# Eight tiles of the second block computed in seven products instead of eight

## What is computed

```
scale = cond @ norm_w.T + 1.0
h = x * (scale * rsqrt(mean(x*x) + EPS))          # x: 4 x 1024 x 512
val, gate = split(h @ up_w.T)                     # up_w: 4096 x 512
h = val * gelu(gate)                              # exact gelu, 2048 wide
h = act_quant(h)                                  # per row: 127 / max|h|, rounded
y = h @ weight_quant(down_w).T + x                # scale 1 / mean|down_w|, rounded to -1, 0, 1
```

## Time and profile before

| what | value |
|---|---|
| median of 3 runs | 761.38 us |
| the profiled execution's own time | 760.18 us |
| its span | 758.4 us |
| PE busy | 736.5 us (97%) |
| DVE busy | 546.8 us (72%) |
| ACT busy | 344.9 us (45%) |
| POOL busy | 96.1 us (13%), all of it before 245 us |

### The profile page before, as it was taken

How to read it: one execution, slowest core, us unless ns; L and a number is a source line. 1 busy time by engine, 2 the same in 40 slices (tenths; PEclk the granted TensorE clock), 3 DMA queues, 4 the chain that set the end, 5 groups by cost and what they waited for, 6 DMA issues and landing times.

```text
span 758.4 us, 15668 instructions
## 1 busy us (share of the span) xinstructions
PE 736.5 (97%) x6190; PEld 611.2 (81%) x6218; DVE 546.8 (72%) x1070; ACT 344.9 (45%) x672; POOL 96.1 (13%) x134
## 2 busy tenths in 40 slices
PE   3999999999999999999999999999999999999998
PEld 2888889888678887888768887788878887688864
DVE  5567777887688776878667775777758776377747
ACT  4788766444255442554235432444315343233325
POOL 0101377773323000000000000000000000000000
PEclk9999999999999999999999999999999999999999
DMA  8787674656546444343533435343343333453302
GB/s 313 275 277 224 197 258 139 223 170 220 207 133 192 152 148 154 115 140 99 175 124 115 129 113 166 105 149 127 126 160 101 99 98 115 130 170 98 103 29 83
DMA packets 43785, 116.63 MB, mean 154 GB/s; under 512 B 4928, under 2 KB 5184, under 8 KB 42432
## 3 DMA queue, kind: packets, MB, share of 16 engines
q1 hardware_dynamic: 43712, 115.63, 46.9%
HBM read 98.83 MB, written 16.78 MB: 152 GB/s over the span
## 4 chain that ended last, share of the span: by engine, by line
PE 85%; DVE 5%; ACT 3%; issue 3%; DMA 2%; POOL 0%; SPq 0%; DVEq 0%; ACTq 0%
PE ps_v L519 15%; PE ps_v L520 15%; PE ps_v L521 15%; PE ps_y L613 12%; PE ps_g L520 8%; PE ps_g L521 8%; PE ps_g L519 8%; PE ps_v L677 1%; DMA q<-in_up_t_dram 1%; DMA sums<-in_up_t_dram 1%; ACT w_hi L758 1%; DVE x_lo L999 1%; ACT g L720 1%; ACT w_hi L763 1%; DVE xt L975 1%
## 5 line engine op out<-in xcount | busy, mean ns | idle before, releaser
L519 PE MATMUL ps_v<-x_hi,w_hi 128*128 128x256 f16 x1216 | 332.0, 273 | 5.3 <-DVE x_lo L999 2.4
L521 PE MATMUL ps_v<-x_hi,w_lo 128*128 128x256 f16 x1216 | 332.0, 273 | 0.0
L520 PE MATMUL ps_v<-x_lo,w_hi 128*128 128x256 f16 x1216 | 332.0, 273 | 0.0
L519 PE MATMUL ps_g<-x_hi,w_hi 128*128 128x256 f16 x640 | 174.6, 273 | 0.0
L520 PE MATMUL ps_g<-x_lo,w_hi 128*128 128x256 f16 x640 | 174.5, 273 | 0.0
L521 PE MATMUL ps_g<-x_hi,w_lo 128*128 128x256 f16 x640 | 174.4, 273 | 0.0
L702 ACT COPY ps_g<-ps_v 128x256 f32<-128x256 f32 x96 | 34.3, 357 | 231.7 <-PE ps_v L521 231.7
L519 PEld LDWEIGHTS ps_v<-x_hi,w_hi 128*128 128x128 f16 x1216 | 119.2, 98 | 23.3 <-DVE ps_g L1005 2.8
L520 PEld LDWEIGHTS ps_v<-x_lo,w_hi 128*128 128x128 f16 x1216 | 119.1, 98 | 16.0
L521 PEld LDWEIGHTS ps_v<-x_hi,w_lo 128*128 128x128 f16 x1216 | 119.2, 98 | 14.0
L713 ACT ACTIVATE g<-ps_g,w_unscale 128x512 f32<-128x512 f32 x128 | 87.3, 682 | 68.2 <-PE ps_g L521 68.1
(11 more groups left out here) (109 smaller groups left out, 579.4 us busy)
## 6 DMA issues: line engine op xcount, KB each, us to landing
w_lo<-w_lo_dram SPq DMA_DIRECT2D x96, 448.0 KB, 3.3
q<-in_up_t_dram SPq DMA_DIRECT2D x16, 512.0 KB, 5.4
xt<-in_x_cols_dram SPq DMA_DIRECT2D x8, 1024.0 KB, 5.1
res<-in_x_rows_dram SPq DMA_DIRECT2D x26, 256.0 KB, 3.5
out_dram<-res SPq DMA_DIRECT2D x26, 256.0 KB, 2.8
sums<-in_up_t_dram SPq DMA_DIRECT2D x12, 512.0 KB, 4.8
xs<-in_x_rows_dram SPq DMA_DIRECT2D x22, 256.0 KB, 3.5
w_lo_dram<-w_lo SPq DMA_DIRECT2D x16, 256.0 KB, 4.8
```

Source lines behind the costliest of these rows:

```text
L519: pe.matmul(to, w_hi[:, wh:wh + P], hi, start=start and kt == 0, stop=False, skip_group_check=True)
L520: pe.matmul(to, w_hi[:, wh:wh + P], lo, start=False, stop=False, skip_group_check=True)
L521: last = pe.matmul(to, w_lo[:, wl:wl + P], hi, start=False, stop=(kt == 1), skip_group_check=True)
```

## The change

Four things change.

**Seven products from tile 24 on** (`S_FIRST` = 24 in place of 32). The activations of block 1 get their sums (`made(1)` has eight operands, three low parts and four differences more on DVE, four high parts more on ACT, in steps 9 to 15), and tiles 8 to 15 of the weight sums come first (`SUM_ORDER`), at steps 14 to 24, the other eight at steps 25 to 33. Sixteen sums as before.

**Memory.** The down weights' raw parts move from `sums` to the part of `w_lo` that holds sums of weights, so `sums` is free from the start and POOL does sums and down parts in turn (`DOWN_AT`). The third place of a sum is `res`. `load_xt(2)` moves from step 14 to 16, and the 1 MB of rows of block 3 are loaded behind it in one piece into `q`, in place of four loads of 256 KB.

**Head.** The first block's rows are loaded in two halves, one more of their sums of squares goes from DVE to ACT, `weight_high(0)` comes before `weight_bound(1)`, two low parts are made on POOL (`low_first`), `weight_scale(1)` comes before `low(0, XB21)`, and the products of tile 0 are reordered.

**Bounds.** The turn of a weight's peak is a bf16 matmul against a bf16 identity in place of an fp32 transpose, and `weight_bound(j)` waits for the clamp, not for the turn.

```diff
-    SUM_AT = (20, 21, 22, 23, 24, 25, 26, 27, 28, 30, 31, 33, 34, 36, 37, 39)
-    SUM_PLACE = (2, 3, 0, 2, 1, 0, 3, 1, 0, 1, 0, 1, 0, 1, 0, 1)
+    S_FIRST = J + J // 2
+    SUM_ORDER = (*range(J // 2, J), *range(J // 2))
+    SUM_AT = (14, 15, 17, 18, 20, 21, 23, 24, 25, 26, 27, 28, 29, 30, 32, 33)
+    SUM_PLACE = (0, 1, 0, 1, 0, 1, 0, 1, 2, 0, 1, 2, 0, 1, 0, 1)
...
     def in_seven(n):
-        return n >= 2 * J
+        return n >= S_FIRST
...
+        if c == 1:
+            return (XB11, XB12, XT1, XT2, XT3, XB21, XB22, XN4)
...
-    LOAD_DOWN_AT = (10, 10, 11, 11, 11, 12, 12, 14, 15, 16, 17, 17, 18, 18, 18, 19)
-    LOW_DOWN_AT = (12, 13, 14, 15, 15, 16, 16, 16, 17, 17, 18, 18, 18, 19, 19, 20)
+    LOAD_DOWN_AT = (11, 11, 10, 10, 11, 12, 12, 14, 15, 15, 16, 16, 17, 18, 18, 18)
+    DOWN_AT = (11, 11, 12, 12, 13, 14, 15, 15, 15, 16, 17, 18, 18, 18, 19, 20)
+    LOW_DOWN_AT = (12, 13, 13, 14, 14, 15, 16, 16, 16, 17, 18, 19, 19, 19, 20, 21)
...
-        down_raw = [res[:, 0, :], res[:, 1, :], *[sums[:, k * D:(k + 1) * D] for k in range(4)],
+        down_raw = [res[:, 0, :], res[:, 1, :], *[w_lo[:, k * WL + WA:(k + 1) * WL].bitcast(F32) for k in range(LS)],
...
+        xs_fourth = q[:, 8 * TB:16 * TB].bitcast(F32)
...
-            return {1: 1, 2: 9, 3: J - 1, 4: 2 * J + 11}.get(c, (c - 2) * J + 6) + i
+            return {1: 1, 2: 9, 3: J + 1, 4: 2 * J + 11}.get(c, (c - 2) * J + 6) + i
...
-                if n == J - 2:
+                if n == J:
                     load_xt(2)
+                    sp.wait_ge(w_ready, J)
+                    sp.dma_start(xs_fourth, x_rows[3]).then_inc(xs_fourth_loaded, 16)
...
-                turn(j % 2, peak[:, j % 2:j % 2 + 1]).then_inc(w_rows, 1)
+                pe.matmul(ps_y[:, 1, (j % 2) * P:(j % 2 + 1) * P], peak_top[:, j % 2:j % 2 + 1].to_broadcast([P, P]),
+                          ident_top, start=True, stop=True).then_inc(w_rows, 1)
...
             def sum_high(k):
+                j = SUM_ORDER[k]
                 act.wait_ge(s_step, 4 * (k + 1))
-                act.wait_ge(val_ready, J + min(k + 2, J))
+                act.wait_ge(val_ready, j + 2 if J + j + 1 >= S_FIRST else J + j + 2)
...
             square(0, 0)
             square(0, 1)
+            square(0, 2)
             weight_bound(0)
+            weight_high(0)
             weight_bound(1)
-            weight_high(0)
...
+            low_first(XB12)
+            low_first(XB22)
-            for n in range(J):
+            for n in range(SUM_AT[-1]):
...
-            for k in range(J):
-                sum_weights(k)
+                for k in range(J):
+                    if n + 1 == SUM_AT[k]:
+                        sum_weights(k)
+                for k in range(J):
+                    if n == DOWN_AT[k]:
+                        quantize_down(k)
...
+                    if j == 9:
+                        difference(1, XT1)
+                        difference(1, XT2)
                     if j == 10:
                         low(1, XB11)
                         low(1, XB12)
                     if j == 11:
+                        difference(1, XT3)
+                        low(1, XT1)
+                    if j == 12:
+                        difference(1, XN4)
+                        low(1, XT2)
+                    if j == 13:
+                        low(1, XT3)
                         low(1, XB21)
+                    if j == 14:
                         low(1, XB22)
+                    if j == 15:
+                        low(1, XN4)
```

More of the change, by code:

```diff
@@ L210, in bass_cond_norm_geglu_bitlinear @@
         up_loaded = [sem(f"up_loaded{k}") for k in range(RS)]
-        sum_loaded = [sem(f"sum_loaded{k}") for k in range(4)]
+        sum_loaded = [sem(f"sum_loaded{k}") for k in range(3)]
         down_sum_loaded = [sem(f"down_sum_loaded{k}") for k in range(4)]
@@ L325, in sum_raw @@
             place = SUM_PLACE[k]
[L326 to L329, removed]
+            if place == 2:
+                return res[:].rearrange("p a n -> p (a n)")
+            return sums[:, place * WS:(place + 1) * WS]
         def sum_loads(k):
@@ L375, in load_lo @@
                 if in_seven(n):
-                    if n < 2 * J + LS:
-                        last = max(k for k in range(J) if SUM_PLACE[k] == 2 + (n % LS) // 2)
-                        sp.wait_ge(ws_ready, last + 1)
-                    if n < 3 * J:
-                        stored, count = sum_store(j)
+                    if n < S_FIRST + LS:
+                        sp.wait_ge(dw_ready, LS + 6 + n % LS)
+                    if n < S_FIRST + J:
+                        stored, count = sum_store(SUM_RANK[j])
                         sp.wait_ge(stored, count)
@@ L438, in _ @@
             sp.dma_start(norm_sb, norm_t).then_inc(consts_loaded, 16)
-            sp.dma_start(xs_first, x_rows[0]).then_inc(xs_first_loaded, 16)
+            for half in range(2):
+                sp.dma_start(xs_first[:, half * 2 * D:(half + 1) * 2 * D],
+                             x_rows[0][:, half * 2 * D:(half + 1) * 2 * D]).then_inc(xs_first_loaded[half], 16)
             load_up(0)
@@ L536, in direct_first @@
                 product(n, OA11, XB11, ps_g[:, n % NG, :], 0, start=True)
+                if n == 0:
+                    product(n, OA21, XB12, ps_v[:, n % NV, :], 1)
                 product(n, OA11, XB12, ps_g[:, n % NG, :], 1)
@@ L734, in square @@
                     tile = xs_third[:, i * D:(i + 1) * D]
+                elif c == 3:
+                    act.wait_ge(xs_fourth_loaded, 16)
+                    tile = xs_fourth[:, i * D:(i + 1) * D]
                 else:
@@ L812, in _ @@
                     if j == 10:
+                        high(1, XT1)
+                        high(1, XT2)
+                    if j == 11:
+                        high(1, XT3)
                         high(1, XB21)
+                    if j == 12:
                         high(1, XB22)
+                    if j == 13:
+                        high(1, XN4)
+                if n == S_FIRST + 1:
+                    high(2, XN4)
                 for k in range(J):
@@ L826, in _ @@
                         high(b + 1, XB22)
-                        high(b + 1, XN4)
+                        if b >= 2:
+                            high(b + 1, XN4)
                 for c in range(1, NB):
@@ L978, in difference @@
             def difference(c, k):
-                before = (c - 2) * 4
+                before = (c - 1) * 4
                 if k == XT1:
@@ L1093, in _ @@
             dve.tensor_scalar(cs[:], cs_raw, cs_scale[:], None, ALU.mult).then_inc(cs_scaled, 1)
-            for i in range(2, TT):
+            for i in range(3, TT):
                 tile = xs_first[:, i * D:(i + 1) * D]
-                dve.wait_ge(xs_first_loaded, 16)
+                dve.wait_ge(xs_first_loaded[i // 2], 16)
                 dve.scalar_tensor_tensor(out=tile, in0=tile, scalar=1.0, in1=tile, op0=ALU.mult, op1=ALU.mult,
@@ L1105, in _ @@
             low(0, XB11)
-            low(0, XB12)
             norm(0, 2)
             norm(0, 3)
+            weight_scale(1)
             low(0, XB21)
-            low(0, XB22)
             for n in range(NJ + 2):
@@ L1115, in _ @@
                     row_scales(b - 1)
-                if b == 0 and j + 1 < J:
+                if b == 0 and 1 <= j < J - 1:
                     weight_scale(j + 1)
```

90 lines of the change are left out of this document (57 added, 33 removed).

## The result

The changed kernel takes 771.06 us (median of 4 runs, 770.25 to 772.19) against 760.93 us for the kernel before (4 runs): ratio 1.014, 95% interval 1.0128 to 1.0152. It is 10.1 us slower. The forecast was 761.7 with a range of 755.8 to 766.0, so it was wrong, and on the slow side. The profiled execution took 770.89 us, with a span of 768.8 in place of 758.4.

The account below looks back on a forecast made before the run. PE bounds the kernel before; VectorE in steps 14 to 31 would turn PE's 7.0 us gain into waits. PE 1.9 us later at tile 32, less 1.6 after, gives + 0.3: 760.5 profiled, median 761.7, range 755.8 to 766.0.

Parts of the forecast that it names:

- The head and the bounds: Tile 0's earlier start was to give 1.0 us, the cheaper turns of bounds in block 0 0.7 us.
- The saving of the seven products: On PE, eight tiles at 4.58 in place of 5.24 us a step: 5.3 us less PE work.
- After step 32: Waits for `seed_gate` and `second_val` in steps 35 to 39 go, - 1.6 us; 1.1 before the maximum's transposes stays.
- start of step 14 at 93.1, step 24 at 149.3, step 32 at 195.1: Forecast starts of VectorE's steps in us; before the change 94.64, 149.52 and 194.60.
- Start of step 14: VectorE starts step 14 with PE's gain of 1.7 us less 0.2 for differences and low parts: 93.1.
- Steps 14 to 23: VectorE: three more sums + 4.3 us, a low part + 0.6, an idle wait gone - 3.6; step 24 at 149.3.
- Steps 24 to 31: VectorE takes 45.8 us: 45.1, + 1.6 for `seed_gate` and `second_val`, - 0.9 for a `sum_high` wait.
- Rival 3: Sums come late in consecutive steps 23 to 30, each step 0.2 to 0.9 longer: + 3.5 us, about 765; chance 0.28.
- Rival 1: PE keeps its gain as VectorE's steps shrink by themselves: 8.6 us faster, median about 753; chance 0.12.
- Rival 2: Half the gain: VectorE's waits for `absolute` absorb more work and sums cost 1.2: - 4 us, median 757.5; chance 0.17.
- rival 4: The change doesn't reach its steps; something waits for the moved 2 MB behind step 16: + 1 to + 5 us; chance 0.05.
- wrong in the slow direction: Sign: VectorE or ACT wait for `sum_high` or POOL's `s_step` in steps 17 to 30 for over 2 us together.

Follow-up runs that it names:

- head_bounds: The kernel before with only the head and the bounds of the change: 759.51 us, against 760.77 for the kernel before.
- both_off: The changed kernel with POOL's sums and down parts on 16 columns and a memset for each sum's low part: 753.20 us.
- pool_thin: The changed kernel with POOL's instructions of the sums and down parts on 16 columns in place of 256 and 512: 757.74 us.
- pool_downs_thin: The changed kernel with only POOL's down parts on 16 columns, the sums whole: 765.90 us.
- warm_29_2: The changed kernel with 40 unused matmuls of 256 columns on PE ahead of the product that waits 5.5 us: 769.25 us.
- before_pool_thin: The kernel before with POOL's sums and down parts on 16 columns: 758.48 us, against 760.63 for the kernel before.

## Why the prediction was wrong

**What held.** The head and the bounds: tile 0 starts at 15.76 (15.7 was said; 15.6 to 16.2 in the other traces with this head), and head_bounds gains 1.3 us where 1.7 was said. The saving of the seven products (both_off). That VectorE, not PE, sets the time of steps 24 to 31, and that it turns PE's gain into waits: the longest is for `second_val` at step 28 to 29, as said; for `second_val` and `seed_gate` together PE waits 8.0 us (6 to 8 were said). After step 32 nothing more is lost, and of the waits of the earlier trace rows after 205 us only the 1.1 before the maximum's transposes is left.

**The step that failed** is the chain "start of step 14 at 93.1, step 24 at 149.3, step 32 at 195.1". It came out 9.9 us too short, in three pieces:

- *Start of step 14: 95.09 against 93.1, + 2.0.* The clamp of the weight's peak stands behind POOL's down parts; from 80 to 95 us POOL is busy 10.5 of 15 us, where it was 6.3. The timeline of POOL in the changed kernel, and the turn on PE that waits for it:

```profile
86.03 1.45 POOL L928 TENSOR_SCALAR res<-res 128x512 f32<-128x512 f32 x1
87.58 1.13 POOL L920 TENSOR_SCALAR w_unscale<-p,cs_unscale 128x1 f32<-128x1 f32 x1
88.80 0.52 POOL L913 TENSOR_SCALAR peak_top<-peak 128x1 bf16<-128x1 f32 x1
```

```profile
89.37 0.23 PE L605 MATMUL ps_y<-x_lo,peak_top 128*128 128x128 bf16 x1 [1.16 <-POOL peak_top L913]
```

  POOL is held up as well: this down pass takes 1.45 us in place of 0.61 (its neighbours at 84.55 and 90.19), and an instruction on one element 1.13 in place of 0.30 (its mean in the kernel before). VectorE's step 12 takes 6.1 us in the changed kernel, and 5.0 in pool_thin and in pool_downs_thin, where PE doesn't wait for the clamp: so 1.1 of the 2.0 come with the down parts ahead of the clamp, most likely through its lateness (VectorE's instructions in this step are longer too). The other 0.9 isn't parted; step 12 itself starts only 0.9 us earlier than before, and the starts of such traces differ by as much. The forecast had named what VectorE does in steps 9 to 13 and nothing of POOL's clamp.
- *Steps 14 to 23: 59.9 us against 56.2, + 3.7.* PE waits 1.2 us for the norm at tile 16, as the forecast had it in size though for another operand, and 2.3 us for `hidden` at tile 20, where a short wait was named. The sums were costed with POOL beside them (1.45 for 1.28). That the same lock would lengthen maxima, `rounded`, differences and low parts more than it already did was not.
- *Steps 24 to 31: 50.0 us against 45.8, + 4.2.* Step 28 takes 187.57 - 176.67 = 10.9 us where 9 were said. `rounded` of two tiles takes 1.73 in place of 0.75 and the sum 1.75 in place of 1.28 (pool_thin); behind it PE's half clock costs 1.8 us (warm_29_2).

The whole can be divided with the kernels in which POOL is thin. The table has VectorE's busy time, of each stretch between the starts of `hidden` (from the windows of the traces, in us).

| stretch | before: length, busy | before_pool_thin: busy | after: length, busy | pool_thin: busy |
|---|---|---|---|---|
| steps 14 to 23 | 54.21, 42.80 | 36.03 | 59.26, 50.33 | 40.94 |
| steps 24 to 31 | 45.08, 38.04 | 33.44 | 50.00, 44.23 | 38.06 |

What POOL adds is the busy time less that with thin POOL. In steps 14 to 23 it was 42.80 - 36.03 = 6.8 and is 50.33 - 40.94 = 9.4; in steps 24 to 31 it was 4.6 and is 6.2. Together it grew by 4.2 us. The forecast held 3 x 0.17 = 0.5 of this growth, so 3.7 of the 7.9 us that it missed from step 14 on are the lock's. The waits for `sum_high` are 2.1 us where it counted none. VectorE waits 1.5 us for PE up to 194 and 196 us, in and just behind the stretch at half clock, where it counted none either. The rest, by difference 0.6, fits what `seed_gate` and `second_val` didn't find room for: in steps 24 to 31 VectorE's own work grew by 38.06 - 33.44 = 4.6 us, and the waits for `absolute` fell only from 5.6 to 3.3. With the 2.0 ahead of step 14 this makes the 9.9. It is a division by subtraction, good to some tenths. What experiments show directly is the whole: with POOL's columns gone, step 32 starts at 191.87.

**The term** is thus the lock between VectorE and POOL: 3.7 us of longer instructions and up to 1.1 of a late clamp, about half of the miss, the largest part but not all of it. The forecast saw the lock (the 4.1 us of `rsqrt`, the sum of 1.75) and let it decide only the price of three sums, with 1.66 as the upper end. It should have gone over every SBUF-only form in the steps where POOL's new work lands, and over what waits for POOL. The overlap was wrong beside it: with PE's reserve gone and VectorE the bound, late sums and a slow PE each added to the chain, where the forecast let them cost nothing. POOL is busy 85.6 us from 80 to 205 us, and was 73.1 from 80 to 195.

**The rivals.** Rival 3 named 765 and the right side, but its mechanism carries little: sums that come late cost VectorE 2.1 us together, most of it in steps 17 and 18 (1.8) and not in the row of sums from 23 to 30, and POOL itself mostly waited for loads (27.4 us for those into `sums`). Rival 1 would be true with VectorE relieved (753.20). Rival 2 and rival 4 found nothing: no instruction waits for the moved 2 MB behind step 16 in the changed kernel, though with thin POOL VectorE waits 2.3 us for an `xt` load. The sign for "wrong in the slow direction" was the wait for `sum_high` or `s_step` above 2 us; at 2.1 it was just met, and was not the main reason.

**Best version.** head_bounds, 759.51 us, beats both kernels: the head and the bounds without the moved sums.

## What to carry to other kernels

When work is added to POOL beside a VectorE that sets the pace, cost it on VectorE too: look for one instruction form with two lengths in the trace, take the shortest as its own price, and charge the difference to every form with its tensors in SBUF alone, the 4-element ones as well, for each stretch that POOL will newly fill. The forms with one tensor in PSUM were free of it here. The shortest in one trace can itself be stretched; a run with POOL's instructions made thin gives the real price, instruction by instruction. And ask whether there is still room to hide it: 11.7 us of such excess cost the kernel before 2.15 us, while PE set its time, and 15.4 cost the changed kernel 13.3. Before work is moved to an engine with a low average share, read its share in the very window: ACT, at 46% over the span, was already at 9.30 of 12 us from 88 to 100 us, and full with the passes added.

## What the hardware showed unexpectedly

- Tiny instructions pay the most. A piece of the square root takes 0.16 us alone and 0.57 to 0.67 beside POOL; `rsqrt` as a whole takes 4.0 us (183.56 to 187.57) against 2.3 in pool_thin (173.99 to 176.32). In the kernel before the small instructions of steps 14 to 31 carry 5.0 of the 11.7 us.
- POOL loses as well: a down pass of 0.61 us took 1.45, and 16 columns in pool_thin took a mean of 0.27 to 0.44 us in its larger groups, where passes of the same size that met no long instruction of VectorE took 0.20 and 0.28 (in pool_downs_thin, from 84.9 us).
- In a wait of 5.5 us TensorE fell to 1.2 GHz (from 187 to between 193 and 194), and 40 filler matmuls gave back about 2 us. The same drop came right behind a wait of 2.3 us, with full clock again between 135 and 136.
